# A pad of 448 bytes in front of the large SBUF buffers cut to 64 bytes

## What is computed

```python
x = x + mamba(_layernorm(x))     # projection, 4-tap convolution, state-space scan, gate, group norm, projection
x = x + ffn(_layernorm(x))       # silu(x W1') * (x W3') then W2, each weight with a rank-16 LoRA term

# inside mamba, with H=128 heads of P=64, N=128 states, G=8 groups
proj = x @ in_proj_w.T                       # gate, (x, B, C), dt
xBC  = silu(conv4(xBC) + conv_b)
y    = ssd(x, A, B, C, D, softplus(dt + dt_bias))   # intra-chunk scores with decay, states carried over chunks
g    = y * silu(gate)                        # then group rms norm over 1024 channels, times norm_w
out  = g @ out_w.T
```

## Time and profile before

| | |
|---|---|
| median of 3 runs | 1948.89 us (1945.69 to 1950.14) |
| the profiled execution's own time | 1950.14 us |
| its span, first to last instruction | 1948.3 us |
| mean granted TensorE clock | 0.971 of full speed |
| busy share | PE 93%, PE weight load 75%, DVE 62%, ACT 59%, POOL 55% |
| moved by DMA | 205.94 MB, 106 GB/s on the mean |

### The profile page before, as it was taken

One profiled execution on the slowest core, in us unless ns is written; L12 is line 12 of the kernel. 1 busy time (PEld: TensorE's weight loads), 2 busy tenths in 40 slices (PEclk: granted clock), 3 DMA queues, 4 the chain that ended last, 5 costly groups with the idle time before them and its releaser, 6 DMA issues.

```text
span 1948.3 us, 31241 instructions
## 1 busy us (share of the span) xinstructions
PE 1814.8 (93%) x9826; PEld 1456.0 (75%) x9826; DVE 1200.2 (62%) x2070; ACT 1143.7 (59%) x2185; POOL 1066.2 (55%) x989
## 2 busy tenths in 40 slices
PE   5879999999899999998999989998999997779999
PEld 4658787878777877787778778887887786557867
DVE  5457677766576758675867676667766776622112
ACT  4666667666667666666666666666666764322111
POOL 3346666666566656665656565655666664431221
PEclk9989999999999999999999999999999998779999
DMA  3523334333433343433433343334333532221101
GB/s 119 152 88 119 101 120 145 119 102 120 140 114 107 114 131 103 123 98 117 132 101 119 113 147 106 115 103 135 99 124 93 158 93 77 70 72 43 30 21 44
DMA packets 118770, 205.94 MB, mean 106 GB/s; under 512 B 23889, under 2 KB 28369, under 8 KB 118577
## 3 DMA queue, kind: packets, MB, share of 16 engines
q1 hardware_dynamic: 118576, 203.62, 34.2%
HBM read 198.85 MB, written 4.72 MB: 104 GB/s over the span
## 4 chain that ended last, share of the span: by engine, by line
PE 74%; DVE 11%; issue 5%; POOL 4%; ACT 3%; DMA 2%; SPq 0%; DVEq 0%; POOLq 0%; ACTq 0%
PE bank L1280 14%; PE bank L1282 13%; PE bank L1281 13%; PE bank L1343 6%; PE bank L1381 4%; PE bank L1382 4%; PE bank L1383 4%; PE bank L1356 4%; PE bank L1369 3%; DVE ow_l L1074 3%; PE bank L1321 3%; DVE x_ch L1068 2%; DMA w_raw<-in_wp 2%; DVE xdt L1087 1%; DVE bcT L1068 1%
## 5 line engine op out<-in xcount | busy, mean ns | idle before, releaser
L596 POOL TENSOR_TENSOR w_l<-w_raw,w_h 128x512 fp32r<-128x512 f32 x288 | 373.4, 1300 | 312.8 <-ACT w_h L726 311.3
L1280 PE MATMUL bank<-x_h,w_h 128*128 128x512 f32 x1160 | 470.4, 406 | 24.5 <-DVE bcT L1068 11.3
L1281 PE MATMUL bank<-x_l,w_h 128*128 128x512 f32 x1160 | 455.5, 393 | 0.0
L1282 PE MATMUL bank<-x_h,w_l 128*128 128x512 f32 x1160 | 455.2, 392 | 0.0
L1068 DVE SCALAR_TENSOR_TENSOR x_ch<-bank,par,x_ch 128x511 f32<-128x511 f32 (+2 forms) x384 | 287.2, 748 | 120.8 <-ACT x_ch L743 111.8
L774 ACT ACTIVATE decay<-decay,cols 128x128 f32<-128x128 f32 x1024 | 317.0, 390 | 0.7
L1280 PEld LDWEIGHTS bank<-x_h,w_h 128*128 128x128 f32 x1160 | 219.9, 190 | 86.1 <-issue 25.9
L602 POOL TENSOR_SCALAR_AFFINE_SELECT decay<-decay 128x512 f32<-128x512 f32 x256 | 200.0, 795 | 127.7 <-DMA decay<-cum_scratch 127.7
L1282 PEld LDWEIGHTS bank<-x_h,w_l 128*128 128x128 f32 x1160 | 219.7, 189 | 48.2
L1281 PEld LDWEIGHTS bank<-x_l,w_h 128*128 128x128 f32 x1160 | 220.3, 190 | 41.6
L1381 PE MATMUL bank<-ow_h,gT_h 128*128 128x512 f32 x512 | 226.0, 441 | 16.2 <-POOL gT_l L620 16.2
(11 more groups left out here) (135 smaller groups left out, 2851.0 us busy)
## 6 DMA issues: line engine op xcount, KB each, us to landing
w_raw<-in_wp SPq DMA_DIRECT2D x288, 256.0 KB, 3.6
decay<-cum_scratch SPq DMA_DIRECT2D x256, 256.0 KB, 3.8
ec<-ecum_scratch SPq DMA_DIRECT2D x96, 256.0 KB, 4.7
ow_raw<-in_ow SPq DMA_DIRECT2D x64, 256.0 KB, 4.8
raw<-in_w SPq DMA_DIRECT2D x20, 256.0 KB, 2.8
w_raw<-in_w SPq DMA_DIRECT2D x10, 256.0 KB, 3.5
acc<-in_x SPq DMA_DIRECT2D x8, 256.0 KB, 4.7
out<-acc SPq DMA_DIRECT2D x8, 256.0 KB, 2.0
```

What stands on the lines that cost most here:

```text
L596: pool.tensor_tensor(w_l[:, s, :], w_raw[:, s, :], w_h[:, s, :].bitcast(F32), ALU.subtract).then_inc(wl_ready, 1)
L1280: pe.matmul(dst, wh, xh, start=(k == 0), stop=False)
L1281: pe.matmul(dst, wh, xl, start=False, stop=False)
L1282: last = pe.matmul(dst, wl, xh, start=False, stop=(k == len(terms) - 1 and not more))
```

## The change

The pad `align` shrinks from 112 to 16 floats in each partition.

```diff
         mean_sq, rstd = sb("mean_sq", [P, 1]), sb("rstd", [P, 1])
-        sb("align", [P, 112])
+        sb("align", [P, 16])
 
         scan_ctx = ExitStack()
```

## The result

The change made the kernel slower: 1957.95 us (median of 5 runs, 1957.22 to 1965.29) against 1947.64 us (median of 5, 1944.51 to 1950.14). The medians are 10 us apart; the ratio of all runs is 1.0066 with a 95% interval of 1.0043 to 1.009, which is 8 to 18 us. The forecast was 1948.5 us with a range to 1955.5.

A forecast was written before the change was run, and what follows sets the result against it. The prediction took PE's stream of matmuls to bound the kernel. PE's pace 0, elementwise engines 0 and loads -0.5 us, against the median of 1948.89 us, gave 1948.4, rounded to 1948.5 us, with an 8-in-10 range of 1942.5 to 1955.5.

The forecast's parts named there:

- The pace of PE: PE's matmul stream: start-to-start distance stays at 0.23 us whatever the addresses, so the term is 0.
- The cover of 40 ns: PE's weight load of 188 ns hides beside a 0.23 us matmul distance, with some 40 ns to spare.
- The bound: PE's matmuls of 587 against 592 ns differ by 0.8%; over PE's 1442 us of the chain, 12 us either way.
- The third rival: Buffer starts count in a way no row shows, above all on PE's two streams; 3.5 us per ns, either way; chance 0.05.
- Elementwise engines: ACT, DVE and POOL operations: start address changes nothing, 0, with a bound of 3.5 us to either side.
- Loads: DMA loads into moved buffers such as w_raw and decay: 0.5 us gained, between 0 and 1.0.
- blocks of 256 bytes: Loads: an aligned 2048-byte row touches 8 blocks instead of 9, so a load might land 0.10 us earlier.
- the first rival: Loads get shorter and it is felt, through the chain's DMA and POOL's waits for decay: 1942 us; chance 0.18.
- The count of beats: Loads: the skill's rule, applied to writes, takes a row from 68 beats to 64, 6% per row, giving 1945 us.
- The second rival: Shifted loads make POOL's masks hold DVE's ow_l longer at 7 group starts: 7 us more, 1956 us; chance 0.17.

The follow-up runs named there:

- e1: Kernel before the change with 32 floats put ahead of x_h, so everything starts 128 bytes higher: 1947.75 us, ratio 0.9997.
- e2: Kernel before the change with x_h, x_l and all else ahead of the pad 128 bytes higher, the rest in place: 1961.02 us, ratio 1.0070.
- e5: Kernel before the change with only w_l and w_raw moved to the remainder 256 by 512: 1955.71 us, ratio 1.0049.
- e10: Kernel before the change with w_h alone moved to the remainder 256 by 512: 1961.39 us, ratio 1.0077.
- e14: Kernel before the change with only gT_h and gT_l, weights of the output product, moved to the remainder 256: 1955.35 us, ratio 1.0038.
- e13: Kernel before the change with only sgT and x_ch 384 bytes lower, nothing that PE's split products read: 1947.65 us, ratio 0.9997.
- e9: Kernel before the change with x_l, acc, xn, ident and small vectors moved to the remainder 256, x_h and the weights kept: 1953.87 us, ratio 1.0037.
- e4: Kernel before the change with the pad at 48 floats, so weights minus moving operand is 256 bytes: 1949.35 us, ratio 1.0011.

## Why the prediction was wrong

The step that failed is "The pace of PE", with the value 0. The runs showed 228.1 ns growing to 232.7 in its place, which is 16 us on the projection and 2 on the feed-forward part, and that the distance between moving operand and weights is what it goes by (e1, e2, e5, e10, e14).

- **The fact was there, and I read past it.** I wrote that the change moves w_h and w_l against x_h and x_l, and then asked whether PE is slowed by what the others do. It is not (e13, and the quiet stretches at 1797 and 1803 us). The partner is PE's own reading of the weights, which I had asked only for its length.
- **The evidence for 0 could not show it.** I compared the pace at 1051 us with that at 1900 us and called the second "another pair of addresses". Both pairs lie at distance 0 by 256, as every other large pair in the kernel before; the order of allocation gave this, and the earlier trace rows could not speak for a distance that no large pair has. And a single distance read 0.23 us, with a step of 10 ns, where 4.6 ns on 3480 matmuls are 16 us.
- **The cover of 40 ns was no cover.** The weight load still takes 188 ns after the change (L1281, PEld) and stays inside the distance. What grew is the stream that it meets.
- **The bound was no bound on this.** The 0.8% between 587 and 592 ns gave 12 us to either side, and a range that had taken it in would have held the result, but by luck. `b2T` and `a2T` too are at distance 0 by 256 from each other, so this pair says nothing of other distances, and the pace then grew by 2.0%, the median duration of L1281 by 1%. The third rival named the mechanism in one half sentence and got 0.05.
- **Elementwise engines: right.** The ACT copy of b2T takes 612 ns after (614 before), now off the multiple of 512, and the busy times agree to 1 us.
- **Loads: right that they don't reach the end, and blocks of 256 bytes don't count.** `w_raw` lands in 3.4 us after and `decay` in 3.7 (3.6 and 3.8 before), and POOL waits 126.9 us for `decay` (127.7), which looks like the first rival's sign. But in e1, where the same buffers also start on multiples of 256, they land in 3.6 and 3.9, POOL waits 133.6, and the DMA share of the middle stretch is 0.39, as it is 0.38 before and after. The count of beats in the Trainium skill, "DMA: Bandwidth & Descriptors", section "How a descriptor splits into AXI transactions", shows in no write here. The first rival falls.
- **The second rival fell too.** `ow_l` has a median of 1112 ns (1114 before) and PE's weight loads wait 2.6 us for it (3.2 before). The result has the sign and nearly the size of this rival, 1956 us, and nothing of its cause.

The Trainium skill, "TensorE: Matmul & The Clock Gate", section "Step-by-step: what each phase is for", says that PE has two independent read ports and that loading the next weights takes no SBUF bandwidth from the running matmul. e5 and e14 don't agree that the two are independent: with only the stationary operand moved by 128 bytes, the matmuls that use it or run over its load take 4 to 5 ns (e5) and about 3 ns (e14) longer of 228 to 230. Which part of the way they share, no run here shows.

Open are: what in the SBUF makes 192 bytes better than 128 and 224; whether a load slows the stream before it, the one that it is for, or both; what in the start of a stretch chooses between the two patterns of e9; and how much of the loss the clock gives back as a rule, since one profile of each kernel shows it.

## What to carry to other kernels

Where matmuls follow each other without a gap, the start addresses of the moving operand and of the weights belong to the design: here eight distances were tried, the two that are multiples of 256 bytes were the best, and the others cost 0.8 to 2.5% of the pace. An edit that moves a buffer (a new small tensor, a smaller pad) can change this for every pair behind it, so before costing it at nothing, write down the distance of each pair that PE reads at once, before and after. And a pace must be read over many matmuls: the last digit of a start time is larger than the effect.

## What the runs showed of the hardware

- PE's mean pace of 128x512 matmuls of this kind, at a granted clock of 0.99, is 228 ns when the distance of moving operand and weights is a multiple of 256 bytes (e4, before), 229.9 at 192, and 232.7 to 233.9 at 32, 64, 96, 128 and 224. From the eleventh matmul of a stretch on it is 226.7, 228.6, and 233.2 to 234.0.
- It goes by the distance and not by the place: all 128 bytes higher is 0.9997 of the time, either side alone 1.0066 (the change) and 1.0070 (e2).
- It needs no other engine and no transfer: 227.5 and 232.5 ns stand in stretches in which DVE, ACT, POOL and DMA do nothing.
- After a pair at a bad distance the next pairs at distance 0 are slower too, for some nine matmuls (231.9, 232.9, 233.4 ns and on, against 226.7, in e14). After the small matmuls of L1329 it is the same in the kernel before.
- At a bad distance the pace also depends on how the stretch began: 228.9 or 233.1 ns with the same addresses (e9).
